# A one-core graph-attention layer: exponents of g and p straight from h, a third PSUM bank for h, new orders up to the end of the first group, and closing sums split by value half

## What is computed

```
# N = 4096 rows, 256 features; adj is 4096 x 4096 of 0 and 1
h = relu(layernorm(x)) @ W.T
src = h @ a1
dst = h @ a2
e = leaky_relu(src[:, None] + dst[None, :], negative_slope=0.2)
e = where(adj == 0, -9e15, e)
out = x + softmax(e, axis=1) @ h
```

## Time and profile before

| | |
|---|---|
| median of 3 runs | 384.48 us (384.36 to 384.53) |
| the profiled execution | 384.67 us |
| span of its trace | 382.9 us |
| TensorE busy | 376.8 us, 98% |
| VectorE busy | 363.9 us, 95% |
| ScalarE busy | 195.1 us, 51% |
| GpSimd busy | 42.0 us, 11% |
| granted TensorE clock | 0.999 |

### The profile page before, as it was taken

One profiled execution on the slowest core, in us unless ns is written; L12 is line 12 of the kernel. 1 busy time (PEld: TensorE's weight loads), 2 busy tenths in 40 slices (PEclk: granted clock), 3 DMA queues, 4 the chain that ended last, 5 costly groups with the idle time before them and its releaser, 6 DMA issues.

```text
span 382.9 us, 9216 instructions
## 1 busy us (share of the span) xinstructions
PE 376.8 (98%) x3358; PEld 330.7 (86%) x3358; DVE 363.9 (95%) x458; ACT 195.1 (51%) x271; POOL 42.0 (11%) x66
## 2 busy tenths in 40 slices
PE   8999899999999999999999999999999999999996
PEld 6788688888888888888888888888888888888885
DVE  4999999999999999999999999999987999999965
ACT  5899754744443644344445544444446443444330
POOL 3897020000000001110000002100000012100000
PEclk9999999999999999999999999999999999999999
DMA  7922476847676666776676667766665577766503
GB/s 241 370 78 56 130 235 218 287 154 238 217 236 208 205 220 214 243 229 218 220 223 207 209 217 233 236 222 225 215 205 184 168 222 240 232 220 221 165 2 110
DMA packets 27024, 78.22 MB, mean 204 GB/s; under 512 B 3956, under 2 KB 9336, under 8 KB 27000
## 3 DMA queue, kind: packets, MB, share of 16 engines
q1 hardware_dynamic: 25712, 74.72, 60.9%
q0 software_dynamic: 1280, 3.16, 2.2%
q10 hardware_dynamic: 8, 0.00, 0.0%
HBM read 73.66 MB, written 4.21 MB: 203 GB/s over the span
## 4 chain that ended last, share of the span: by engine, by line
PE 96%; ACT 1%; DVE 1%; DMA 1%; issue 1%; ACTq 0%
PE ps L1390 87%; PE ps L1214 2%; PE ps L1229 2%; PE ps L1235 2%; PE ps L1240 2%; DMA a_rows<-a 1%; PE ps L1179 1%; PE ps L1195 1%; DVE rows_sb L1119 0%; ACT c_row L494 0%; ACT h_sb L468 0%; ACT L620 0%; ACT p_hi L504 0%; ACTq L479 0%; DVE inv_den L1115 0%
## 5 line engine op out<-in xcount | busy, mean ns | idle before, releaser
L1390 PE MATMUL ps<-v_sb,p_hi 128*128 (+2 forms) x2048 | 251.8, 273 | 1.0 <-ACT p_hi L504 0.9
L514 ACT ACTIVATE p_hi<-p_sb,gp 128x1024 f16<-128x1024 f32 x126 | 144.4, 1149 | 166.6 <-DVE p_sb L785 140.0
L1390 PEld LDWEIGHTS ps<-v_sb,p_hi 128*128 128x128 f16 x2048 | 199.6, 98 | 26.9 <-issue 1.2
L792 DVE SCALAR_TENSOR_TENSOR p_lo<-p_sb,gp,p_hi 128x1024 f16<-128x1024 f32 x126 | 160.8, 1277 | 7.1 <-ACT p_hi L514 6.7
L785 DVE SCALAR_TENSOR_TENSOR p_sb<-c_row,gp,adj_sb 128x1024 f32<-128x1024 uint32 (+1 forms) x126 | 160.5, 1278 | 0.0
L1390 PE MATMUL ps<-v_sb,p_lo 128*128 (+1 forms) x1024 | 142.7, 273 | 0.0
L1390 PEld LDWEIGHTS ps<-v_sb,p_lo 128*128 128x128 f16 x1024 | 100.0, 98 | 12.7 <-DVE p_lo L792 0.2
L452 POOL DMA_DIRECT2D out<-rows_sb x24 | 13.0, 541 | 263.1 <-DVE rows_sb L1086 262.9
L401 POOL TENSOR_SCALAR hn_sb<-x_sb,moments,rstd 128x256 f32<-128x256 f32 x17 | 21.3, 1261 | 4.3 <-DVE rstd L734 3.4
L744 DVE SCALAR_TENSOR_TENSOR hnt_lo<-ps,hnt_hi 128x256 f16<-128x256 f32 x32 | 12.9, 410 | 0.5 <-ACT hnt_hi L484 0.5
L1229 PE MATMUL ps<-w_hi,hnt_hi 128*128 128x258 f16 x64 | 12.5, 277 | 0.5 <-ACT h_sb L468 0.4
(11 more groups left out here) (85 smaller groups left out, 87.3 us busy)
## 6 DMA issues: line engine op xcount, KB each, us to landing
adj_sb<-adj_t SPq DMA_DIRECT2D x128, 512.0 KB, 4.8
x_sb<-x SPq DMA_DIRECT2D x7, 512.0 KB, 8.3
out<-rows_sb POOLq DMA_DIRECT2D x24, 128.0 KB, 4.3
c_row<-c_flat SPq DMA_DIRECT2D x3, 512.0 KB, 6.1
out<-rows_sb SPq DMA_DIRECT2D x8, 128.0 KB, 1.7
x_sb<-x SPq DMA_DIRECT2D x2, 256.0 KB, 3.8
c_row<-s_flat SPq DMA_DIRECT2D x1, 512.0 KB, 3.8
w_nat<-w SPq DMA_DIRECT2D x1, 256.0 KB, 2.8
```

What stands on the lines that cost most here:

```text
L514: nc.scalar.activation(p_hi[:, u % R, :], p_sb[:, u % R, :], ACT.Copy, scale=p_scale[:, bass.ds(t, 1)])\
L792: nc.vector.scalar_tensor_tensor(out=p_lo[:, u % R, :], in0=p_sb[:, u % R, :], scalar=p_scale[:, bass.ds(t, 1)], in1=p_hi[:, u % R, :], op ...
L1390: return nc.tensor.matmul(ps[:, k, 0:width], part[:, u % R, k * P:(k + 1) * P], v_sb[:, bass.ds(t, 1), v, 0:width], start=start, stop=stop ...
```

## The change

- `banks_h = (6, 7, 4)` takes the place of two banks: h is projected into three PSUM banks in turn, and `project_hi(t)` waits for tile t - 3. The bound's scratch banks move (`bank_d` 4 to 5, `bank_e` 5 to 2).
- `gp_args` is gone. ScalarE makes g and p's scale straight from the kept dst column: `exp_g` with scale and bias of the bound, `exp_p` with a quarter of them. VectorE makes one 1-column `p_bias` instead. GpSimd makes a fourth column of `exp_scale`, and makes it after most of its other work of the first stage.
- The lists of who normalises and who makes the high values are new (GpSimd: 16 tiles and 13 pairs, where it had 17 and 5), and the written orders of all four engines are new up to the end of the first group. The three runs of filler matmuls (`keep_busy`) stay.
- In the last group the closing sums first do all products with high values of a block (six matmuls, after which the denominator is complete, `den_summed`), and later the three with low values. VectorE inverts the denominators in between. Block 4 is scaled by ScalarE, gets x added by GpSimd, and is stored from ScalarE's queue.

```diff
-    BY_VECTOR = [26]
+    BY_VECTOR = [24]
...
-    HIGH_BY_GPSIMD = [0, 4, 8, 10, 12]
+    HIGH_BY_GPSIMD = [0, 2, 4, 6, 8, 10, 12, 14, 16, 22, 26, 28, 30]
...
-        bank_w, bank_n, bank_d, bank_e = 4, 1, 4, 5
-        bank_h = 6
+        bank_w, bank_n, bank_d, bank_e = 4, 1, 5, 2
+        banks_h = (6, 7, 4)
...
-            for n, factor in enumerate((-0.8, 0.8, -0.8 * H_DOWN)):
+            for n, factor in enumerate((-0.8, 0.8, -0.8 * H_DOWN, 0.2)):
...
+            pool.wait_ge(row_scaled, 1)
+            nc.gpsimd.tensor_tensor(rows_sb[:, SIDE_ROW, 0:F], rows_sb[:, SIDE_ROW, 0:F], x_sb[:, FIRST_OF_LAST + SIDE_ROW, :],
+                                    ALU.add).then_inc(side_row_ready, 1)
...
-            def exp_gp(tiles, n):
-                act.wait_ge(gp_args_ready, n)
-                nc.scalar.activation(gp[:, :, tiles], gp_args[:, :, tiles], ACT.Exp).then_inc(gp_ready, 1)
+            def exp_g(t0, t1):
+                act.wait_ge(c_bias_ready, 1)
+                act.wait_ge(h_kept, t1)
+                nc.scalar.activation(g_col[:, t0:t1], h_sb[:, t0:t1, F + 1], ACT.Exp,
+                                     bias=exp_bias[:, 0:1], scale=exp_scale[:, 1:2]).then_inc(g_ready, 1)
+
+            def exp_p(t0, t1):
+                act.wait_ge(p_bias_ready, 1)
+                act.wait_ge(h_kept, t1)
+                nc.scalar.activation(p_scale[:, t0:t1], h_sb[:, t0:t1, F + 1], ACT.Exp,
+                                     bias=p_bias[:, 0:1], scale=exp_scale[:, 3:4]).then_inc(p_scale_ready, 1)
...
-            dve.wait_ge(scales_ready, 5)
+            dve.wait_ge(scales_ready, 6)
...
+            def last_inverse(k, k1):
+                b, b1 = FIRST_OF_LAST + k, FIRST_OF_LAST + k1
+                dve.wait_ge(den_summed, k1)
+                nc.vector.tensor_scalar(den[:, b:b1], ps[:, k:k1, F], den_scale[:, 0:1], DEN_TINY,
+                                        ALU.mult, ALU.max).then_inc(den_taken, k1 - k)
+                dve.wait_ge(den_taken, k1)
+                nc.vector.reciprocal(inv_den[:, b:b1], den[:, b:b1]).then_inc(last_inverse_ready, k1 - k)
...
+                def high_values(k):
+                    for u in range(U - closing, U):
+                        if k == 0:
+                            pe.wait_ge(p_lo_ready, n + (u + 1))
+                        product(u, t + u, k, p_hi, 0, False, False)
+                        done = product(u, t + u, k, p_lo, 0, False, False)
+                    done.then_inc(den_summed, 1)
+
+                def low_values(k):
+                    pe.wait_ge(den_taken, k + 1)
+                    for u in range(U - closing, U):
+                        done = product(u, t + u, k, p_hi, 1, False, u == U - 1)
+                    done.then_inc(rows_done, 1)
+
+                high_values(0)
+                high_values(1)
+                high_values(2)
+                high_values(3)
+                low_values(0)
+                low_values(1)
+                high_values(4)
+                high_values(5)
+                low_values(2)
+                low_values(3)
+                high_values(6)
+                low_values(4)
+                high_values(7)
+                low_values(5)
+                low_values(6)
+                low_values(7)
```

More of the change, by code:

```diff
@@ L991, in _ @@
             split_lo(7, 7, 0)
+            value_lo(12)
+            dve.wait_ge(c_col_ready, 1)
+            nc.vector.transpose(c_blocks[:], c_col[:]).then_inc(c_blocks_ready, 1)
             dve.wait_ge(p_lo_ready, 6)
@@ new lines, in high_sums @@
+            def high_sums(t, m):
+                k0, k1 = PARTS[t][m]
+                _, last, count = parts_of(PARTS, t, m)
+                if m == 0:
+                    pe.wait_ge(v_ones_ready, 1)
+                    pe.wait_ge(v_lo_ready, t // 2 + 1)
+                if last:
+                    pe.wait_ge(p_hi_ready, t + 1)
+                else:
+                    pe.wait_ge(part_hi_ready[t], count)
+                for k in range(k0, k1):
+                    if t == 0 and k in banks_h:
+                        pe.wait_ge(*kept(max(i for i in range(T) if banks_h[i % HB] == k)))
+                    product(t, t, k, p_hi, 0, t == 0, False)
+                    product(t, t, k, p_hi, 1, False, False)
@@ new lines, in low_sums @@
+            def low_sums(t, m):
+                k0, k1 = LOW_PARTS[t][m]
+                _, last, count = parts_of(LOW_PARTS, t, m)
+                if last:
+                    pe.wait_ge(p_lo_ready, t + 1)
+                else:
+                    pe.wait_ge(part_lo_ready[t], count)
+                for k in range(k0, k1):
+                    done = product(t, t, k, p_lo, 0, False, False)
+                if last:
+                    done.then_inc(slot_free, 1)
+            keep_busy(banks_h[0], 3)
@@ new lines, in _ @@
+            turn(0)
+            turn(1)
+            project_hi(0)
+            project_hi(1)
+            turn(2)
+            project_w_lo(0)
+            project_w_lo(1)
+            project_lo(0)
+            project_hi(2)
+            turn(3)
+            project_w_lo(2)
+            project_lo(1)
+            turn(4)
+            project_lo(2)
+            turn(5)
+            project_hi(3)
+            project_w_lo(3)
+            project_hi(4)
+            project_w_lo(4)
+            project_lo(3)
@@ new lines, in _ @@
+            spread_d()
+            project_hi(28)
+            project_w_lo(28)
+            turn_d()
+            project_lo(28)
+            project_hi(29)
+            project_w_lo(29)
+            project_hi(30)
+            project_w_lo(30)
+            project_hi(31)
+            project_lo(29)
+            project_lo(30)
+            project_w_lo(31)
+            project_lo(31)
+            high_sums(0, 0)
+            high_sums(0, 1)
+            high_sums(0, 2)
+            high_sums(0, 3)
```

697 lines of the change are left out of this document (335 added, 362 removed).

## The result

The changed kernel takes **385.04 us** (median of 18 runs, 384.83 to 385.83), the kernel before 384.44 in the same comparison. The ratio is 1.0016 with a 95% interval from 1.0009 to 1.0022: slower by 0.6 us, where 1.3 less was forecast. Two of the 18 executions of the kernel before, at 490.63 and 561.18, are left out of the ratio as slow ones; why they were slow is not known. The profiled execution took 385.35 with a span of 383.7.

The account below looks back on a forecast made before the run. The prediction took TensorE to bound the kernel, with gains only where it stands idle: 0.75 + 0.25 + 0.2 + 0.28 = 1.48 us, taken as 1.4, giving a median of 383.1 us, range 382.4 to 384.3.

Parts of the forecast that it names:

- What bounds the kernel: Whole kernel: TensorE, busy 98%; gains only before the third column tile (5.1 us idle) and behind the last matmul.
- The lead at the start: Start of the first stage: TensorE 3.5 pairs further when it turns tile 6, at 13.45; gain 0.75 us.
- The dense part: First stage up to the bound: the lead survives and 0.25 of TensorE's 0.75 us idle is also gained.
- From the bound to the third tile: From `exp_bias` to the third column tile: fewer ScalarE and VectorE steps and short waits gain 0.2 us.
- no wait on `p_lo`: Sign in the first group: TensorE would not wait for the low halves that VectorE makes.
- The end: Behind the last matmul: last denominators inverted during nine low-value matmuls; gain 0.28 us, 0.44 at most.
- The side row: Block 4's new path at the end: GpSimd's add takes 1.25 us, its store covered by 0.25 us or more.
- the same queue later: Rival, first stage: GpSimd's tiles cost 1.375 each, its queue ends at 39.2, total 385.1; chance 0.12.
- The rival of the starved first group: Tiles 15 to 29: VectorE falls behind and the lead is given back; gain 0.4, total 384.1; chance 0.13.
- same: Outcome for the whole kernel: a change under about 0.77 us, not told from no change; stated chance 0.22.
- slower: Outcome for the whole kernel: the change makes it slower; stated chance 0.13.
- the front's forecast gain of 1.2: Everything ahead of the third column tile: terms of 0.75, 0.25 and 0.2 us.

Follow-up runs that it names:

- closing_alone: The kernel before with only the new closing sums and last rows of the change: 383.99 us against 384.52, ratio 0.9988.
- the two runs: The kernel before with only the new end, 383.99 against 384.52 us; and the changed kernel with the old end put back, 385.74 us.
- three_kinds: The kernel before with 18 unread GpSimd steps added in the first group (six casts, six `tensor_scalar`, six additions): 390.7 us in its one run.

## Why the prediction was wrong

- **What bounds the kernel**: right. Nearly all of the change lies ahead of column tile 3 and behind the last matmul. The 3000 matmuls between took 329.48 (50.83 to 380.31), 0.24 more than before. That is the front's doing, since the trace of closing_alone has 329.25. TensorE has a gap of 0.07 ahead of the low half's matmuls of tile 17, at 89.4, just behind the VectorE step that makes that half (88.19 to 89.46); there the prediction saw the half come level with its use. The first column tile of the second group takes 2.96 in place of 2.81; what it waits for is open.
- **The lead at the start**, 0.75 us: right in kind and about in size. Tile 6 is turned with 20 pairs issued at 13.72 (forecast 13.45), and the last batch's reciprocal comes 0.8 earlier. One pair of traces fixes this only roughly: it is at 27.83 to 28.40 in eight of the nine traces with the new front and at 29.04 to 29.26 in the three with the old one.
- **The dense part**, where the prediction went wrong: "VectorE gets one `value_lo` more before the bound, 0.60 us", set off against the two low halves to "about nothing". The 0.60 was read at 88.47, in a stretch where GpSimd does nothing beside it. The trace of the kernel before also has `value_lo` steps of 0.60 beside a GpSimd `tensor_scalar` (at 32.01, 33.27 and 34.61), so a busy GpSimd alone does not lengthen that step; the trace has none that a cast holds up. Here three of the six have casts in their way. The sum put GpSimd's new casts into GpSimd's list alone, as time of an engine with its own queue, and left out what they cost the engine next to them: 1.23 us before the bound. `exp_bias` came at 38.30 for a forecast 37.1; with the casts moved it came at 37.05, and `project_lo` of tile 27 at 34.75 for a forecast 34.8 (35.71 in the changed kernel).
- **From the bound to the third tile**, which is column tile 3: the assumption that VectorE keeps up was wrong by the same cause, 0.70 at the low parts of tile 0, so that "no wait on `p_lo`" failed with 0.40. The small exponentials were sized by the 0.10 of `exp_gp`, which is given neither a scale column nor a bias column; they take 0.28 each. That turned a gain of 0.15 into a loss of 0.20.
- **The end**: forecast 0.28, measured 0.37 in the traces and 0.5 to 0.7 by the medians of the two runs, whose intervals include 0.37. The side row's add took 0.73, not 1.25, so its store was covered. The Trainium skill (GPSIMD Engine Reference, section 3.1), whose figure gave an estimate of 0.55 plus dispatch, was nearer than my row.
- **The rivals**: "the same queue later" named 385.1, close to the measured time, but by another mechanism. It wanted `exp_bias` to wait for GpSimd, and no such wait is there. The rival of the starved first group did not come true beyond the 0.07 at tile 17. The forecast used the neighbours' contention for one side only, what VectorE does to a GpSimd tile, and not the other way round.
- **The chances**: by their own list "same" adds up to 0.10 + 0.13 = 0.23 and "slower" to 0.12, not 0.22 and 0.13. That changes nothing.

The misses close: 1.93 for five casts and 0.35 for the exponentials are 2.3 of the 2.4 us between the front's forecast gain of 1.2 and its measured loss of 1.2; the 0.24 behind column tile 3 is a third miss, and the sum closes only to a few tenths. With the casts moved, the kernel is at 383.14 to 383.22. That this is next to the forecast 383.1 owes something to luck, since the exponentials and the 0.24, both missed, and the end, sized too small, roughly cancel.

## What to carry to other kernels

When work is handed to an idle GpSimd, price it twice: its own time, and 0.35 to 0.5 us for each cast or addition that falls on a VectorE step with two SBUF operands, if VectorE is on the path there (the prices are from casts of 128x512 and additions of 128x256). Put such work beside VectorE steps that read PSUM, or on ScalarE. A duration read where the neighbour engine was idle, or busy with another kind of step, is a lower bound, not the price.

## What the runs showed of the hardware

- Beside GpSimd's casts of 128x512, VectorE's two-operand steps of 2 x 256 columns (`value_lo`) went from 0.60 to 1.01 us and those of 512 columns (`p_lo`) from 0.66 to 1.02, from start to start; steps with one operand in PSUM (`hnt_lo`, 0.33 from start to start, as at 38.62 in the changed kernel) kept their time.
- A VectorE `tensor_scalar` on four strided values, with scale and bias columns from SBUF, went from 0.29 to 0.57 and 0.64 beside casts. It has one SBUF tensor only, so two tensor operands are not the only steps that a cast holds up.
- GpSimd's `tensor_scalar` of 128x256 fp32 is stretched the most (1.235 to 3.07 us) and holds VectorE up the least (0.17); the addition of two tensors, 0.73 alone, holds it up the most (0.47). Both figures are from the one run of three_kinds.
- ScalarE's small exponentials with scale and bias columns take 0.28 from start to start, one without them 0.10. They also read four strided values of `h_sb`, the other eight packed ones. That stride is the cause is unlikely: `std<-moments`, also strided, with one such column, lasts 0.30, between their 0.38 and the 0.20 of the one without.
